# Sharing the low weight parts between VectorE and a ScalarE pass with a GpSimd subtraction

## What is computed

```python
x = x + tanh(g_xattn) * attention(layernorm(x), ctx, ctx, mask, Wq, ..., bo)   # 16 heads, 154 keys
x = x + tanh(g_ffn)   * experts(layernorm(x), Wg, W1, b1, W2, b2)              # 8 experts, top 2
# experts: S = sigmoid(xt @ Wg); G, I = top_k(S, 2)
#          h = gelu(xt @ W1 + b1);  y = h @ W2 + b2;  out = sum of the two chosen y times G
```

## Time and profile before

| what | value |
|---|---|
| time, three runs | median 541.58 us (541.09 to 541.70) |
| the profiled execution | 543.22 us |
| its span | 541.40 us |
| busy over the span: TensorE, VectorE, ScalarE, GpSimd | 81%, 60%, 40%, 32% |
| busy in 110.0 to 155.9 us (frames 2 and 3): TensorE, VectorE, ScalarE, GpSimd | 37.66, 36.68, 25.11, 6.83 us |

### The profile page before, as it was taken

How to read it: one execution, slowest core, us unless ns; L and a number is a source line. 1 busy time by engine, 2 the same in 40 slices (tenths; PEclk the granted TensorE clock), 3 DMA queues, 4 the chain that set the end, 5 groups by cost and what they waited for, 6 DMA issues and landing times.

```text
span 541.4 us, 10997 instructions
## 1 busy us (share of the span) xinstructions
PE 435.9 (81%) x4070; PEld 337.3 (62%) x4070; DVE 323.4 (60%) x789; ACT 217.3 (40%) x542; POOL 170.8 (32%) x163
## 2 busy tenths in 40 slices
PE   6457567878878879974156999999999999999980
PEld 3334224545545435543155999999999999999970
DVE  5756686788787876663870555545545555555540
ACT  2131553465565545740000644444444444444420
POOL 8613501020221212100002155455355445445231
PEclk9766978999999989985555899999999999999995
DMA  7433322262453533421001023223223223223211
GB/s 208 97 127 104 98 92 63 89 196 87 123 152 101 146 94 120 149 77 39 1 0 39 22 40 51 50 42 50 51 40 49 51 41 48 53 41 45 37 21 19
DMA packets 33065, 40.03 MB, mean 74 GB/s; under 512 B 8351, under 2 KB 27667, under 8 KB 33011
## 3 DMA queue, kind: packets, MB, share of 16 engines
q0 software_dynamic: 12608, 27.32, 22.2%
q1 hardware_dynamic: 17873, 11.11, 7.3%
q10 hardware_dynamic: 2532, 0.89, 0.7%
HBM read 25.71 MB, written 9.44 MB: 65 GB/s over the span
## 4 chain that ended last, share of the span: by engine, by line
PE 63%; DVE 21%; DMA 6%; issue 4%; ACT 3%; POOL 1%; SPq 0%; ACTq 0%; DVEq 0%; POOLq 0%
PE bank L1175 7%; PE bank L1159 7%; PE bank L1161 6%; PE bank L1160 6%; PE bank L1176 6%; PE bank L1177 6%; PE bank L944 4%; DVE rowmax L658 4%; DMA W_stage<-in_L_ffn_W 3%; PE bank L1091 3%; PE bank L982 3%; PE bank L1113 3%; PE bank L961 2%; DVE W L676 2%; DVE stats L605 2%
## 5 line engine op out<-in xcount | busy, mean ns | idle before, releaser
L1159 PE MATMUL bank<-xh,W 128*128 128x128 f16 x624 | 122.0, 221 | 0.9 <-DVE xl L862 0.9
L1160 PE MATMUL bank<-xl,W 128*128 128x128 f16 x624 | 122.0, 221 | 0.0
L1161 PE MATMUL bank<-xh,W 128*128 128x128 f16 x624 | 121.9, 221 | 0.0
L573 ACT ACTIVATE h<-bank,b1T 128x128 f32<-128x128 f32 x312 | 89.2, 368 | 70.3 <-PE bank L1161 68.7
L413 POOL DMA_INDIRECT out_rows<-y_sb,scatter_tab x39 | 63.8, 1637 | 114.9 <-DVE y_sb L876 108.6
L1175 PE MATMUL bank<-W,hh 128*128 x312 | 85.4, 274 | 0.0
L1176 PE MATMUL bank<-W,hh 128*128 x312 | 85.0, 273 | 0.0
L1177 PE MATMUL bank<-W,hl 128*128 x312 | 85.0, 273 | 0.0
L868 DVE CAST hh<-h 128x512 f16<-128x512 f32 x78 | 34.4, 441 | 81.5 <-ACT h L573 81.4
L658 DVE TENSOR_REDUCE rowmax<-bank 128x2 f32<-128x308 f32 x128 | 56.8, 473 | 23.2 <-PE bank L961 21.5
L519 ACT ACTIVATE probs<-bank 128x512 f32<-128x512 f32 x80 | 47.1, 595 | 48.8 <-PE bank L1039 37.9
(11 more groups left out here) (179 smaller groups left out, 684.8 us busy)
## 6 DMA issues: line engine op xcount, KB each, us to landing
W_stage<-in_L_ffn_W POOLq DMA_DIRECT2D x32, 512.0 KB, 4.2
xn_scratch<-attn SPq DMA_DIRECT2D x8, 256.0 KB, 2.2
qst<-qh SPq DMA_DIRECT2D x60, 32.0 KB, 2.4
X_late<-in_x SPq DMA_DIRECT2D x6, 256.0 KB, 4.8
out_rows<-X_late SPq DMA_DIRECT2D x6, 256.0 KB, 2.5
qst<-ql SPq DMA_DIRECT2D x28, 32.0 KB, 2.5
xg<-xn_scratch,gather_tab POOLq DMA_INDIRECT x39, 3.0
out_rows<-y_sb,scatter_tab POOLq DMA_INDIRECT x39, 3.9
```

Of the source, the lines that this page charges most:

```text
L573: ins = nc.scalar.activation(h32[s % 4][:, m * P:(m + 1) * P], H_BANKS[s % 4][:, m * P:(m + 1) * P], ACT.Gelu_apprx_tanh, scale=1.0 / W_SC ...
L1159: nc.tensor.matmul(dst, wh, xh[t % 3][:, cut], start=(c == 0), stop=False)
L1160: nc.tensor.matmul(dst, wh, xl[t % 3][:, cut], start=False, stop=False)
L1161: ins = nc.tensor.matmul(dst, wl, xh[t % 3][:, cut], start=False, stop=(c == KC - 1))
```

## The change

The 28 low parts of the frames are shared out in turn. Odd chunks stay as they are. Each even chunk (4, 6, ... 30) goes the way of the setup's chunks: ScalarE does its second pass in place right behind the first, then GpSimd subtracts, then GpSimd issues the load of chunk n + 2. VectorE skips these chunks. The semaphore `w_setup_ready` becomes `w_pool_ready`, with counts for each chunk.

```diff
+        ON_POOL = [n < SETUP_CHUNKS or n % 2 == 0 for n in range(len(chunks))]
+        pool_nth = [sum(ON_POOL[:n + 1]) for n in range(len(chunks))]
+        dve_nth = [n + 1 - pool_nth[n] for n in range(len(chunks))]
...
-                if n < SETUP_CHUNKS:
+                if ON_POOL[n]:
+                    if n == E * KC:
+                        pool.wait_ge(kst_late_made, 1)
+                    if n >= len(chunks) - 4:
+                        pool.wait_ge(pv_done, ITEMS * UNITS_PER_BATCH)
                     pool.wait_ge(w_high, n + 1)
-                    nc.gpsimd.tensor_tensor(low, W_stage[n % 2][:, :], high, ALU.subtract).then_inc(w_setup_ready, 1)
+                    nc.gpsimd.tensor_tensor(low, W_stage[n % 2][:, :], high, ALU.subtract).then_inc(w_pool_ready, 1)
                 if n + 2 < len(chunks):
-                    if n < SETUP_CHUNKS:
-                        pool.wait_ge(w_setup_ready, n + 1)
+                    if ON_POOL[n]:
+                        pool.wait_ge(w_pool_ready, pool_nth[n])
                     else:
-                        pool.wait_ge(w_ready, n + 1 - SETUP_CHUNKS)
+                        pool.wait_ge(w_ready, dve_nth[n])
                     load(n + 2)
...
                 ins = nc.scalar.activation(chunks[n][1], W_stage[n % 2][:, :], ACT.Copy, scale=W_SCALE)
-                if n < SETUP_CHUNKS:
+                if ON_POOL[n]:
                     ins = nc.scalar.activation(W_stage[n % 2][:, :], W_stage[n % 2][:, :], ACT.Copy, scale=W_SCALE)
...
-                if n == E * KC:
+                if n >= E * KC:
                     dve.wait_ge(kst_late_made, 1)
-                if n == len(chunks) - 4:
+                if n >= len(chunks) - 4:
                     dve.wait_ge(pv_done, ITEMS * UNITS_PER_BATCH)
...
                     if i >= 1 and i - 1 in W_SLOTS[u]:
-                        weights_low(SETUP_CHUNKS + w_steps.index((u, i - 1)))
+                        n = SETUP_CHUNKS + w_steps.index((u, i - 1))
+                        if not ON_POOL[n]:
+                            weights_low(n)
...
-            pe.wait_ge(w_setup_ready, SETUP_CHUNKS)
-            pe.wait_ge(w_ready, len(chunks) - SETUP_CHUNKS)
+            pe.wait_ge(w_pool_ready, pool_nth[-1])
+            pe.wait_ge(w_ready, dve_nth[-1])
```

More of the change, by code:

```diff
@@ L202, in build @@
         w_staged, w_used, w_ready = [sem("w_staged0"), sem("w_staged1")], sem("w_used"), sem("w_ready")
-        w_high, w_setup_ready = sem("w_high"), sem("w_setup_ready")
+        w_high, w_pool_ready = sem("w_high"), sem("w_pool_ready")
         exp_z_made, chosen_made, ranked = sem("exp_z_made"), sem("chosen_made"), sem("ranked")
```

## The result

| kernel | median, us | executions |
|---|---|---|
| before | 541.34 | 4 |
| changed | 548.14 (546.48 to 549.84) | 4 |

The ratio is 1.0137, 95% interval 1.0112 to 1.0162: the change costs 7.4 us (6.1 to 8.8). It is the ratio of the means (548.15 and 540.74), so it differs a little from that of the medians, which lie 6.8 us apart. The forecast was 545.2, range 541.3 to 548.0, so the sign was right and the time lies outside the range. The profiled execution took 549.84 us, its span is 548.0 us. The last experiment gives a version that is faster than both kernels.

What follows compares the result with a forecast made beforehand. No engine was taken as full; the chain changes engine every microsecond or two. Terms 0.5 - 0.9 + 0.1 + 0.6 + 0 + 0.7 + 0.7 + 1.9 = +3.6 us on 541.58 gave 545.2, range 541.3 to 548.0.

Steps and rivals of the forecast that it cites:

- the term of chunk 20: Chunk 20: subtraction holds a Newton step for 1.82 us, the removed low part gives back 1.13: +0.7 us.
- Blocking, the heart of the forecast: VectorE instructions needing what GpSimd holds wait for its whole instruction, up to 2.13 us; drawn from two trace coincidences.
- The rival in which nothing blocks: Short VectorE steps slip in beside the subtractions everywhere: +0.7 us in sum, 542.3, no change; chance 0.18.
- Chunks 4 and 6: Chunk 4: later exponential delays TensorE, +0.5 us; chunk 6: removed low part saves time before maxima, -0.9 us.
- the rival with a collision there: Chunk 6's subtraction comes ahead of the first norm's last Newton step: frame 0 is 2.1 us longer, 547.3; chance 0.2.
- Chunks 16 and 18: Newton steps held 1.35 us, low part returns 1.13; chunk 18's earlier load offsets its 0.95 us pass: 0 together.
- Chunks 24 and 26: Chunk 24: ScalarE idle by more than a pass, nothing; chunk 26: TensorE's turning covers the pass, nothing, otherwise 0.95 us.
- Chunk 14: Chunk 14: the exponential ends at 139.62 where TensorE took it at 139.05: +0.6 us.
- Chunk 10: Chunk 10: TensorE delayed some 0.7 us, but ScalarE waits later for chunk 11's load: +0.1 us (0 to 0.4).
- Chunk 28: Chunk 28: two exponentials come 0.95 us later, 0.28 goes into ScalarE's wait for load 29: +0.7 us.
- Chunk 30: Chunk 30: second pass +0.95 us, and the subtraction delays Newton steps and the turning by 2.08: +1.9 together.
- Relief decides: Rival: VectorE's relief at the four even low parts on the chain, 5.6 us, outweighs passes of 3.2: 539.2; chance 0.12.

Runs made afterwards that it cites:

- The last experiment: Changed kernel with only chunks 6, 13, 20 on GpSimd; waiting for the layer norm at 13 and 20: 537.13 us, ratio 0.9923; without waits 547.16, 1.0110.
- the variant without collisions: Changed kernel, but GpSimd waits at chunks 20 and 30 for the layer norm, and chunk 21's bias addition comes at 22: 542.48 us, ratio 1.0035.
- the bias alone: Changed kernel with the bias addition put off from chunk 21 to chunk 22: 545.95 us, ratio 1.0086.
- the first experiment: Changed kernel with chunk 20 alone given back to VectorE: 544.96 us, ratio 1.0066.
- the stand put into the kernel before: Kernel before with eight added VectorE reductions behind frame 4's Newton steps: 545.36 us, ratio 1.0062; with four: 541.84 us, ratio 1.0012.
- the kernel with the short subtraction: Changed kernel, but GpSimd subtracts only 32 of 1024 columns of the frames' chunks; ScalarE's second pass stays whole: 543.23 us, ratio 1.0049.

## Why the prediction was right in sign and wrong in size

**The step that failed is the term of chunk 20**: "Subtraction from 175.86 to 177.99; the Newton step of 176.17 stands for 1.82, the low part gives back 1.13: +0.7." Both of its numbers hold: the step is held for 1.68 us, and the removed low part gives back 1.04 (the time from TensorE's product behind the norm to the milestone, 4.39 us in before and 3.35 in the variant without collisions). What is missing is what came behind the step. From the two timelines, counted from the milestone at 168.09 (before) and 167.82 (changed):

| part | us |
|---|---|
| Newton step held beside the subtraction (1.83 - 0.15) | +1.68 |
| normalisation held beside a load's issue and the bias addition (2.39 - 0.73) | +1.66 |
| TensorE takes up the maximum later behind its start (0.52 against 0.25) | +0.27 |
| low part of VectorE gone (4.39 - 3.35) | -1.04 |
| lower clock up to the next milestone (4.89 - 3.35) | +1.54 |
| lower clock behind it (8.47 - 8.07) | +0.40 |
| sum | +4.51 |

The prediction did say of a low part that leaves VectorE which load starts earlier, but not which addition: "The new waits on GpSimd queue only the next bias and loads; these have frames of air, but see chunks 10, 16 and 28." They had air to be late. It did not ask what they hit when they come early. And it priced a stand of TensorE at its length and left the granted clock behind it out of the sum. The size is confirmed by times, not only by one profile: chunk 20 alone back gives 3.8 us, the bias alone 2.8. The three other profiles with both collisions in frame 4 have 27.04, 25.66 and 25.56 us for this stretch, so +4.5 stands for 3.5 to 5.0.

The clock is missing from the sum at two more places of this profile: behind chunk 28 it is 1.5 us and behind chunk 10 about 1.0 (granted clock 0.91 in 104 to 122 us, 1.00 before). These falls can't be added up as the price of the change: the kernel before has one of its own (0.86 in 190 to 214 us, 0.93 after the change), and over 60 to 262 us both have 0.89.

**Blocking, the heart of the forecast, is right, though one of its two rows did not bear on it.** Every Newton step named (frames 3, 4 and 7) is held to the end of the subtraction. But the prediction also took it from the earlier trace rows, where the held instruction is a TENSOR_SCALAR beside a memset. Later profiles show Newton steps beside the same memset, and they run freely, while the normalisation behind them is held. In the first experiment's:

```profile
26.62 1.79 POOL L368 MEMSET b_stage<- 33x2048 f32 x1
26.83 0.17 DVE L627 SCALAR_TENSOR_TENSOR rstd<-newton,rstd 128x6 f32<-128x6 f32 x1
27.63 1.25 DVE L632 TENSOR_SCALAR xn<-X_early,mv,rstd 128x256 f32<-128x256 f32 x2
```

So what GpSimd does counts as well: only the earlier trace rows, a two-operand instruction beside an addition, was a case of the kind forecast. The rival in which nothing blocks falls: it gave +0.7 us, and the kernel in which the two worst collisions are taken away measures +1.9 us (0.5 to 3.3), where the change as it is has +7.4. That rival's sum is thus near what the change costs without its worst collisions, and its condition is what fails. The Trainium skill (SBUF — State Buffer, section "SBUF: two separate sides") describes the shared port pair as an exclusive lock for a whole instruction; the trace agrees, with 0.15 us becoming 1.83 beside 2.12.

**Chunks 4 and 6**: their stretch is shorter, as forecast, but by less than profiles of unchanged code differ there. The subtraction of chunk 6 began at 78.11 and the last Newton step of the first norm at 78.06, 0.17 us long: the margin of 0.05 us held, in this and in six other profiles with this pass, and the rival with a collision there did not come about. **Chunks 16 and 18**: +0.07, forecast 0; right. **Chunks 24 and 26**: -0.02; right. **Chunk 14**: +0.28 for +0.6; all seven profiles in which chunk 14 goes the way of the change have 0.28 or 0.29. **Chunk 10**: right at 0.1, apart from the clock. The +1.07 of the changed kernel's profile is +0.09 in the one of the first experiment. Of the seven profiles with this pass three have a fall of the clock behind it and take 24.20 to 24.29 us, the others 23.31 to 23.48, as do the kernels without the pass (23.22 to 23.46). **Chunk 28**: +0.65 in the profile in which the clock doesn't fall, forecast 0.7. **Chunk 30**: forecast +1.9, +1.13 in the stretch, 3.1 ± 2.1 by time; not refuted. The turning of frame 7's unit was to come 3.5 us later than at 236.74 and came 8.2 later, mostly for chunk 20 and the clock.

**Relief decides** (the faster rival) falls for this change, but not in kind. A low part gone from item 7 is worth 1.0 us where nothing collides, which is what makes the version with three chunks faster. The Trainium skill (Perfetto Trace Analysis, section "Optimizing Scalar/DVE Operations") leaves open whether such a move helps, because of the shared port. Here both answers come out of the same three chunks, 1.0110 and 0.9923, and the order against the layer norm decides between them.

**What stays open.** The second passes alone cost 5.0 us where my terms give 3.8, inside the interval, but at another place than the terms say: the profile has +4.3 us in the stretch of chunks 16 and 18, for which they give 0.95. The parts of the sum don't add simply, since a variant's profile can have a fall of the clock at a place of its own, as that of chunk 28 above. Over all executions the mean granted clock is the same before (0.889) and after (0.889), so in total the change did not buy a slower clock; the +1.94 us for it in frame 4 is a reading of that stretch, backed by the stall put into the kernel before but not isolated from the stand's own length. What decides whether the clock falls behind a stand, the runs don't show.

## What to carry to other kernels

When work moves to GpSimd, write down which VectorE instructions run beside it, also the short ones, and give each that takes two operands from SBUF, or is a TENSOR_SCALAR from SBUF, the whole rest of GpSimd's instruction (what reads PSUM was not held); then ask which of GpSimd's later instructions come earlier and do the same for them. A wait that keeps GpSimd's long instruction behind VectorE's critical little chain can be worth more than the move itself, and GpSimd had the time for it. Move only what is on the path: three chunks at the right item gained 0.8%, and fourteen in turn lost 1.4%.

## What the runs showed of the hardware

- An instruction of VectorE on 128x2 elements takes 0.15 us alone and 1.83 or 1.98 beside a GpSimd subtraction of 2.12 us. A normalisation with one full operand and two per-partition scalars is held as well: 2.39 for 0.73. Row maxima out of PSUM are not: over all profiles they take 0.47 to 0.48 us beside GpSimd's subtractions and additions.
- What is held depends on what GpSimd does. Beside a memset of 1.80 us Newton steps on 128x6 elements take 0.17 us in nine profiles, and a TENSOR_SCALAR is held in all thirteen (1.83 us before).
- The hold can begin before GpSimd's instruction does by the record: in the kernel with the short subtraction the step starts at 172.28, the addition at 172.91, and both end together (174.21 and 174.18). GpSimd was issuing a load at the time. Beside a load's issue with no addition behind it, steps of 0.15 and 0.16 us ran undisturbed, but the first half of a normalisation did not: six times in five profiles it took 0.70 or 0.71 us in place of 0.41 and ended 0.09 us behind the issue, as in frame 3 of the changed kernel (154.64 to 155.35, issue 154.49 to 155.26). In one more profile it took 0.41, and the issue 0.86 in place of 0.77.
- Behind TensorE's stands in frame 4 the granted clock of the next 4 us was 1.00 after 0.88 us (before) and 1.54 us (short subtraction), 0.59 after 1.57 us (four reductions), 0.57 after 1.73 us (bias later), 0.50 to 0.66 after 3.09 or 3.10 us (four kernels), and 0.50 after 3.39 us (eight reductions). The length does not decide alone: behind the 1.01 us of chunk 28 it fell in five profiles of seven. The Trainium skill (TensorE: Matmul & The Clock Gate, Part 1) says that the clock follows how busy TensorE has been; these rows agree in so far as the falls come behind stands.
- The spread between executions of one kernel goes with the granted clock: over 26 executions of before the span correlates with it at -0.59, over 12 of the first experiment at -0.78. A difference of a microsecond or two between single profiles should be looked up in the clock's row before it is explained.
